# Gated feed-forward of a two-layer block: shifted rows fetched one group ahead, statistics between products, last chunk padded to 128 rows

## What is computed

```python
def shift_token(t):
    t1, t2 = jnp.split(t, 2, axis=-1)
    t2 = jnp.pad(t2, ((0, 0), (1, 0), (0, 0)))[:, :-1]
    return jnp.concatenate([t1, t2], axis=-1)
...
x = x + o @ wo
h = shift_token(x)
mu = h.mean(-1, keepdims=True)
var = h.var(-1, keepdims=True)
h = (h - mu) / jnp.sqrt(var + 1e-05) * lg + lb
h = h @ w1 + b1
a, g = jnp.split(h, 2, axis=-1)
h = a * jax.nn.gelu(g, approximate=False)
x = x + h @ w2 + b2
```

## Time and profile before

| what | value |
|---|---|
| runs | 4908.69, 4929.43, 4920.05 us; median 4920.05 |
| span of the profiled execution | 4908.8 us (its own time is not listed apart; the lowest run is 4908.69) |
| TensorE busy | 4331.1 us, 88% |
| VectorE busy | 2249.6 us, 46% |
| ScalarE busy | 1413.8 us, 29% |
| GpSimd busy | 1258.3 us, 26% |
| mean granted TensorE clock | 0.90 of full |
| DMA | 115.02 MB, 23 GB/s |

### The profile page before, as it was taken

How to read it: one execution, slowest core, us unless ns; L and a number is a source line. 1 busy time by engine, 2 the same in 40 slices (tenths; PEclk the granted TensorE clock), 3 DMA queues, 4 the chain that set the end, 5 groups by cost and what they waited for, 6 DMA issues and landing times. The chain is left out here.

```text
span 4908.8 us, 71554 instructions
## 1 busy us (share of the span) xinstructions
PE 4331.1 (88%) x23249; PEld 2982.9 (61%) x23250; DVE 2249.6 (46%) x5734; ACT 1413.8 (29%) x4622; POOL 1258.3 (26%) x1134
## 2 busy tenths in 40 slices
PE   4999999994996499999998989999687899996875
PEld 3676777762664377777775656676343466764442
DVE  4555555552555334333331156666223466664223
ACT  1333333331111222222222234444111244442111
POOL 2333333333223311111111033343101233432000
PEclk9999999996998578777779989999888999998887
DMA  3000000004001200000001010000100000001003
GB/s 102 2 1 2 1 1 1 2 1 154 30 30 64 89 1 1 1 1 1 1 1 55 17 35 6 9 6 6 55 12 9 28 6 9 6 6 52 12 11 104
DMA packets 102500, 115.02 MB, mean 23 GB/s; under 512 B 11384, under 2 KB 92428, under 8 KB 101516
## 3 DMA queue, kind: packets, MB, share of 16 engines
q1 hardware_dynamic: 97292, 98.38, 6.0%
q0 software_dynamic: 4992, 13.64, 0.8%
HBM read 66.91 MB, written 27.26 MB: 19 GB/s over the span
## 5 line engine op out<-in xcount | busy, mean ns | idle before, releaser
L636 ACT ACTIVATE win_probs<-win_score,win_negmax 128x128 f32<-128x128 f32 (+2 forms) x1170 | 464.1, 405 | 1324.3 <-DVE win_negmax L766 1324.3
L396 POOL TENSOR_TENSOR win_probs<-win_probs,win_rsum 128x512 f32<-128x512 f32 (+1 forms) x420 | 422.7, 1007 | 1465.1 <-DVE win_rsum L781 771.7
L766 DVE TENSOR_REDUCE win_negmax<-win_score 128x2 f32<-128x512 f32 (+2 forms) x422 | 283.0, 671 | 945.5 <-PE win_score L522 479.2
L1498 PE MATMUL ffn_hidden<-ffn_hT,ffn_weights_w 128*128 128x512 f32 x640 | 321.0, 662 | 153.3 <-DVE ffn_inner L1590 151.4
L1779 PE MATMUL rot_lin<-rot_weights_w_qkv,rot_hT 128*128 128x512 f32 x816 | 404.9, 619 | 7.5 <-ACT rot_qk L1875 5.5
L1903 ACT ACTIVATE rot_probs<-rot_probs,rot_negmax 128x256 f32<-128x256 f32 x520 | 260.0, 501 | 366.6 <-DVE rot_negmax L1971 366.6
L1498 PEld LDWEIGHTS ffn_hidden<-ffn_hT,ffn_weights_w 128*128 128x128 f32 x640 | 133.7, 214 | 332.7 <-issue 169.8
L794 DVE COPY win_probsT<-win_turned 128x512 f32<-128x512 f32 (+1 forms) x416 | 276.2, 664 | 93.0 <-PE win_turned L532 92.5
L516 PE MATMUL win_score<-win_KT,win_QT 32*128 32x256 f32 x1036 | 294.4, 403 | 0.0
L1817 PE MATMUL rot_score<-rot_KT,rot_QT 64*128 64x256 f32 x1040 | 292.9, 406 | 0.0
L532 PE MATMUL win_turned<-keep_ident,win_probs 128*128 128x128 f32 x1600 | 287.8, 306 | 0.0
(11 more groups left out here) (271 smaller groups left out, 7912.4 us busy)
## 6 DMA issues: line engine op xcount, KB each, us to landing
weights_w<-in_L_ffn_W SPq DMA_DIRECT2D x16, 512.0 KB
scratch_rows_in<-keep_xn SPq DMA_DIRECT2D x1, 5120.0 KB, 16.5
experts_rows<-scratch_rows_in SPq DMA_DIRECT2D x40, 128.0 KB, 2.0
scratch_rows_out<-experts_y POOLq DMA_DIRECT2D x40, 128.0 KB, 2.0
rot_weights_w_qkv<-in_L_ffn_wqkv SPq DMA_DIRECT2D x3, 1536.0 KB, 6.5
rot_h<-keep_xn SPq DMA_DIRECT2D x36, 128.0 KB
rot_h<-keep_xn SPq DMA_DIRECT2D x36, 127.0 KB
keep_xn<-in_L_attn_x SPq DMA_DIRECT2D x4, 1024.0 KB, 9.4
```

The source lines that it names most:

```text
L396: pool.tensor_tensor(mine, mine, bcast(rsum[:, u % 4, 0:heads], [P, heads, keys]), ALU.mult)\
L636: last = act.activation(probs[:, u % 4, i * width:(i + 1) * width], score[u % 4][:, i * width:(i + 1) * width], ACT.Exp, bias=negmax[:, u ...
L766: dve.tensor_reduce(negmax[:, u % 4, 0:heads], score[u % 4][:, 0:heads * keys].rearrange("p (h k) -> p h k", h=heads), AX.X, ALU.max, nega ...
L1498: last = pe.matmul(hidden[m % RING][k][:], w1[:, c, a:a + P], hT[:, c, :], start=(c == 0), stop=(c == KC - 1))
```

## The change

- The gated weights own a tile `h` for the raw shifted rows (`weights.h`, called `raw` in the stage), beside the stage's `h` for scaled rows. Group 0's rows are fetched by the rotary stage before, on SP, between its last two `after` calls, and that stage waits for them at its end. The fetch of group g is issued once group g-1's rows have been scaled (`h_ready`).
- `make_h` is split: `statistics` of group g+1 (it waits for the fetch) after product 2 of group g (counting from 0), `variances` after product 3, `normalise`, from `raw` to `h`, after the last product and before `take_out`.
- `inner`'s last chunk and `w2`'s last chunk are cleared to 128 rows by GpSimd, once per stage each, and `project` reads 128 partitions in every chunk. SP's load of the 42 rows of `w2` becomes the last of the list and waits for the clear; DVE waits for the clear of `inner` before its first statistics.

The diff, with lines between hunks left out:

```diff
@@ -1341,12 +1341,20 @@
             self.w1_rest = s.sb("w1_rest", [P, KC, P])
+            self.h = s.sb("h", [P, TPG, D])
         self.w2 = s.sb("w2", [P, self.chunks, D])
...
-    def load(self, sp, io, done, layer):
+    def load_h(self, sp, X2, g, done):
+        half = D // 2
+        sp.dma_start(self.h[:, :, 0:half], X2[:, bass.ds(g * TPG + 1, TPG), 0:half]).then_inc(done, 16)
+        sp.dma_start(self.h[1:P, :, half:], X2[0:P - 1, bass.ds(g * TPG + 1, TPG), half:]).then_inc(done, 16)
+        sp.dma_start(self.h[0:1, :, half:], X2[P - 1:P, bass.ds(g * TPG, TPG), half:]).then_inc(done, 16)
+    def load(self, sp, io, done, layer, cleared=None):
@@ -1357,10 +1365,12 @@
         if self.gated:
-            loads += [(self.w2[0:REST, whole, :], at(io[pre + "w2"])[whole * P:, :]),
-                      (self.w1_rest[:, :, 0:REST], w1[:, :, whole * P:self.hid]),
-                      (self.w1_rest[:, :, P // 2:P // 2 + REST], w1[:, :, self.hid + whole * P:])]
-        for dst, src in loads:
+            loads += [(self.w1_rest[:, :, 0:REST], w1[:, :, whole * P:self.hid]),
+                      (self.w1_rest[:, :, P // 2:P // 2 + REST], w1[:, :, self.hid + whole * P:]),
+                      (self.w2[0:REST, whole, :], at(io[pre + "w2"])[whole * P:, :])]
+        for i, (dst, src) in enumerate(loads):
+            if self.gated and i == len(loads) - 1:
+                sp.wait_ge(cleared, 1)
             sp.dma_start(dst, src).then_inc(done, 16)
@@ -1418,7 +1428,7 @@
         w1, w2, b1, b2, gain, offset = weights.w1, weights.w2, weights.b1, weights.b2, weights.gain, weights.offset
-        h = s.sb("h", [P, TPG, D])
+        raw, h = weights.h if gated else X2, s.sb("h", [P, TPG, D])
         hT = s.sb("hT", [P, KC, TOK])
@@ -1428,7 +1438,7 @@
         out = [s.ps(f"out{i}") for i in range(2)]
-        next_loaded, h_loaded = s.sem("next_loaded"), s.sem("h_loaded")
+        next_loaded, h_loaded, cleared = s.sem("next_loaded"), s.sem("h_loaded"), s.sem("cleared")
         var_ready, rstd_ready = s.sem("var_ready"), s.sem("rstd_ready")
@@ -1440,20 +1450,12 @@
             def _(sp):
-                def load_h(g):
-                    half = D // 2
-                    sp.dma_start(h[:, :, 0:half], X2[:, bass.ds(g * TPG + 1, TPG), 0:half]).then_inc(h_loaded, 16)
-                    sp.dma_start(h[1:P, :, half:], X2[0:P - 1, bass.ds(g * TPG + 1, TPG), half:]).then_inc(h_loaded, 16)
-                    sp.dma_start(h[0:1, :, half:], X2[P - 1:P, bass.ds(g * TPG, TPG), half:]).then_inc(h_loaded, 16)
-                if gated:
-                    load_h(0)
                 rotary_loads = rotary.load(sp, io, next_loaded, next_layer)
...
                     with sp.Fori(1, NG) as g:
-                        sp.wait_ge(turned_ready.sem, turned_ready.at(g, 0))
-                        load_h(g)
+                        sp.wait_ge(h_ready.sem, h_ready.at(g, 0))
+                        weights.load_h(sp, X2, g, h_loaded)
+                    sp.wait_ge(h_loaded, 48 * (NG - 1))
                 else:
@@ -1466,6 +1468,7 @@
                 if gated:
+                    pool.memset(inner[:, IC - 1, :], 0.0).then_inc(cleared, 1)
                     with pool.Fori(0, NG) as g:
@@ -1506,7 +1509,7 @@
                             last = pe.matmul(out[n % 2][:, 0:D],
-                                             inner[0:rows[m], m, n * P:(n + 1) * P], w2[0:rows[m], m, :],
+                                             inner[:, m, n * P:(n + 1) * P], w2[:, m, :],
                                              start=(m == 0), stop=(m == IC - 1))
@@ -1558,38 +1561,52 @@
-                def make_h(g, first):
+                def statistics(g, later):
+                    if later:
+                        dve.wait_ge(h_loaded, g * 48)
+                    dve.tensor_scalar(raw[0:1, 0, D // 2:], raw[0:1, 0, D // 2:], keep.going[0:1, bass.ds(g, 1)], None, ALU.mult)
+                    dve.drain()
+                    for n in range(TPG):
+                        dve.bn_stats(stats[:, n, :], raw[:, n, :])
+                def variances():
+                    dve.drain()
+                    for n in range(TPG):
+                        dve.bn_aggr(mv[:, n, :], stats[:, n, :])
+                    dve.drain()
+                    dve.tensor_scalar(ve[:], mv[:, :, 1], 1e-5, None, ALU.add).then_inc(var_ready, 1)
+                def normalise(g, first):
                     if gated:
-                        dve.wait_ge(h_loaded, g * 48 + 48)
-                        dve.tensor_scalar(h[0:1, 0, D // 2:], h[0:1, 0, D // 2:], keep.going[0:1, bass.ds(g, 1)], None, ALU.mult)
-                        dve.drain()
-                        for n in range(TPG):
-                            dve.bn_stats(stats[:, n, :], h[:, n, :])
-                        dve.drain()
-                        for n in range(TPG):
-                            dve.bn_aggr(mv[:, n, :], stats[:, n, :])
-                        dve.drain()
-                        dve.tensor_scalar(ve[:], mv[:, :, 1], 1e-5, None, ALU.add).then_inc(var_ready, 1)
                         dve.wait_ge(rstd_ready, g + 1)
-                        for n in range(TPG):
-                            dve.tensor_scalar(h[:, n, :], h[:, n, :], mv[:, n, 0:1], rs[:, n:n + 1], ALU.subtract, ALU.mult)
-                    else:
-                        if not first:
-                            dve.wait_ge(turned_ready.sem, turned_ready.at(g, 0))
-                        for n in range(TPG):
+                    if not first:
+                        dve.wait_ge(turned_ready.sem, turned_ready.at(g, 0))
+                    for n in range(TPG):
+                        if gated:
+                            dve.tensor_scalar(h[:, n, :], raw[:, n, :], mv[:, n, 0:1], rs[:, n:n + 1], ALU.subtract, ALU.mult)
+                        else:
                             t = g * TPG + n
-                            dve.tensor_scalar(h[:, n, :], X2[:, g * TPG + (n + 1), :], keep.mean[:, bass.ds(t, 1)],
+                            dve.tensor_scalar(h[:, n, :], raw[:, g * TPG + (n + 1), :], keep.mean[:, bass.ds(t, 1)],
                                               keep.rstd[:, bass.ds(t, 1)], ALU.subtract, ALU.mult)
...
-                def multiply(g):
+                def multiply(g, m):
+                    dve.wait_ge(gel_ready.sem, gel_ready.at(g, m + 1))
+                    dve.scalar_tensor_tensor(inner[0:rows[m], m, :], hidden[m % RING][0][0:rows[m], :],
+                                             b1[0:rows[m], 0, m:m + 1], gel[0:rows[m], m % 2, :],
+                                             ALU.add, ALU.mult).then_inc(inner_ready.sem, 1)
+                def multiply_and_prepare(g):
                     for m in range(IC):
-                        dve.wait_ge(gel_ready.sem, gel_ready.at(g, m + 1))
-                        dve.scalar_tensor_tensor(inner[0:rows[m], m, :], hidden[m % RING][0][0:rows[m], :],
-                                                 b1[0:rows[m], 0, m:m + 1], gel[0:rows[m], m % 2, :],
-                                                 ALU.add, ALU.mult).then_inc(inner_ready.sem, 1)
+                        multiply(g, m)
+                        if m == 2:
+                            statistics(g + 1, True)
+                        if m == 3:
+                            variances()
+                    normalise(g + 1, False)
@@ -1606,14 +1623,20 @@
-                make_h(0, True)
+                if gated:
+                    dve.wait_ge(cleared, 1)
+                    statistics(0, False)
+                    variances()
+                normalise(0, True)
                 with dve.Fori(0, NG - 1) as g:
-                    make_h(g + 1, False)
                     if gated:
-                        multiply(g)
+                        multiply_and_prepare(g)
+                    else:
+                        normalise(g + 1, False)
                     take_out(g)
                 if gated:
-                    multiply(NG - 1)
+                    for m in range(IC):
+                        multiply(NG - 1, m)
                 take_out(NG - 1)
@@ -1661,6 +1684,7 @@
         next_loaded, zeroed, masking = s.sem("next_loaded"), s.sem("zeroed"), s.sem("masking")
+        cleared, first_rows = s.sem("cleared"), s.sem("first_rows")
         front_loaded, back_loaded = s.sem("front_loaded"), s.sem("back_loaded")
@@ -1700,7 +1724,7 @@
                 load_h(0, 2, back_loaded)
-                following_loads = following.load(sp, io, next_loaded, layer)
+                following_loads = following.load(sp, io, next_loaded, layer, cleared)
@@ -1717,12 +1741,15 @@
                 after(NG - 2, NG - 1, 0)
+                following.load_h(sp, X2, 0, first_rows)
                 after(NG - 1, 0, None)
+                sp.wait_ge(first_rows, 48)
                 sp.wait_ge(back_loaded, 48 * (NG + 1))
...
             def _(pool):
```

(1 more changed line is left out.)

## The result

The median is 4690.02 us over four runs (4680.42 to 4693.27) against 4921.72 us over four of the kernel before (4908.69 to 4929.43); the ratio is 0.9536, 95% interval 0.9520 to 0.9552. The profiled execution has a span of 4678.7 us, 230.1 less than before.

What follows compares the result with a forecast made beforehand. Bound: TensorE's path in both gated stages, with holes of 151.4 us in one, waiting for DVE's products. Savings of 199.6 in stages plus 30.8 at starts, less 0.5 for semaphores, make 230 us: 4920 - 230 = 4690, range 4662 to 4725.

Steps and rivals of the forecast that it cites:

- Steady group: Gated stages, TensorE: with no hole, a lap is hidden part 18.98, project 10.36 and turn 0.88, 30.2 us.
- Padding: Project's products against w2: reading 128 rows instead of 42 saves 1.41 us a group, 22.6 in 16 groups.
- Rival A: Project's products: the padding gives nothing, 42-row records cost for another reason; laps of 31.6 us, time 4713; chance 0.07.
- First group: Each gated stage's start: group 1's fetch queues behind the rotary tables' loads, readable at 3501; TensorE stalls 3.5 us.
- Last loop group: Each gated stage's end: GpSimd's scaling of rotary tables slows DVE's scaling of rows; TensorE stalls 2.7 us.
- Stage: Each gated stage, TensorE's first transpose to last product: 246.0 + 3.5 + 2.7 = 252.2 us; both 504.4, 199.6 less.
- rival B: Gated stages' first and last groups: stalls of 6 and 4.8 us, each hole dropping the clock; 4711; chance 0.12.
- Start: Start of each gated stage: first fetch moved into the rotary stage, DVE begins 15.4 us earlier, 30.8 for two.
- Rival C: DVE's queue before product 4: waiting for the fetch stalls TensorE once it needs more than 22.6 us; slower; chance 0.02.

Runs made afterwards that it cites:

- rows_100: The changed kernel with the product against w2 reading 100 partitions of the last chunk instead of 128, all still cleared; 4670.8 us, one run.
- rows_64: The changed kernel with the product against w2 reading 64 partitions of the last chunk instead of 128, all still cleared; 4715.0 us, one run.
- no_pad: The changed kernel with the product against w2 reading only the 42 written rows of the last chunk again, clears kept; 4716.1 us (0.9594).
- fetch_before_tables: The changed kernel with group 1's fetch issued ahead of the rotary tables' loads at each gated stage's start; stage sum 498.6 us against 504.3.
- tables_after_rows: The changed kernel with GpSimd's scaling of the rotary tables held until the last group's rows are scaled; stage sum 500.2 us against 504.3.
- fetch_at_start: The changed kernel with group 0's rows fetched at the start of the gated stage again; 4718.8 us (0.9590).
- slow_fetch: The changed kernel with a spare copy of the 127-row transfer ahead of each fetch but the first; 4788.4 us (0.9737).
- 2 x 2: Old or new statistics order, with one tile or own tile, padding and early first fetch kept: old order 4872.2 and 4755.5 us, new order 4687.7 and 4690.0.
- in_place: The changed kernel with one tile for raw and scaled rows, each fetch waiting for the transposes, new order kept; 4687.7 us (0.9538).

## Why the prediction was right

Forecast 4690, range 4662 to 4725, measured 4690.02. That it hits to a fraction of a microsecond is luck: the runs of the changed kernel spread over 13 us, those of the kernel before over 21, and the first gated stage's first transposes come anywhere from 3466.55 us (`rows_100`) to 3487.45 (`rows_64`) in kernels that differ in nothing before it. That it is right to some microseconds is not, since each term stands in the trace:

- *Steady group.* Lap 30.2 forecast, 30.12 measured; hidden part 18.89 instead of the 18.98 taken.
- *Padding.* 22.6 forecast; `no_pad` gives 24.3 by laps and 25.5 of stage. The half of project is 5.18 as worked out; the transposes and the hidden records beside it also run slightly closer (17.33 for 40 records, 17.43 before). The size was right because it was taken as a difference of whole halves. The reason beside it, 0.315 us for each short record against 0.216, makes only 8 x 0.1 = 0.8 of the 1.41 a group; the rest was in the full records next to them. The Trainium skill (TensorE: Matmul & The Clock Gate, "Why this matters for your kernels") says that a single matmul of 32 rows takes as long as one of 128. Within a run of 64-row records the trace agrees, 0.216 us each in `rot_score` as in full ones; at the change between short and full it does not: `rows_64` and `rows_100` differ by 0.67 us a half. Rival A is out.
- *First group.* A hole of 3.5 was forecast from the queueing of the fetch behind the tables, readable at 3501; it was readable at 3501.5, with holes of 2.27 and 1.86. The hole was smaller because TensorE came to it 1.3 us later (3481.44 + 20.26 = 3501.70, forecast 3500.4), mostly by a slower first hidden part, which no term foresaw. But in the first stage the half clock came on top (3.35 us from start to start for four records, 1.72 elsewhere), which the forecast did not have there. `fetch_before_tables` confirms that the tables' loads held the fetch.
- *Last loop group.* 2.7 forecast, 2.60 and 2.59 measured, with DVE's scaling begun 3.3 us after the first of GpSimd's six operations (3.5 forecast); `tables_after_rows` confirms it. The Trainium skill (SBUF — State Buffer, "SBUF: two separate sides") says that GpSimd's instructions and some of VectorE's (those in a two-port mode, or with two SBUF inputs) take a shared port pair as a lock for a whole instruction. By that each of the four short instructions would wait for one of GpSimd's, and 6.27 us against 1.37 agrees; that the scaling is of one of these kinds is not shown by any run here.
- *Stage.* 252.2 forecast, 253.1 and 251.1 measured. Of rival B (worse edges) one part shows, in one stage: the clock drop after a hole, 1.8 us.
- *Start.* 15.4 a stage forecast; DVE's wait fell from 18.09 to 2.79, 15.3. `fetch_at_start` loses it again: TensorE waits 15.5 us longer in a stage, 31 in both, 5 come back in the stages, and the time is 27 us (by the ratios) to 29 (by the medians) longer.
- *Rival C.* The mechanism exists and its point was placed to some 1.5 us (22.6, and 24.1 in the group shown): `slow_fetch` passes it with 27.6 us a fetch and loses 98 us. The kernel's own ordinary fetches stay under it: no DVE wait for one in groups 2 to 7.
- *What the prediction did not see.* It counted the own tile and the order as one change. The 2 x 2 above shows that order alone brings the whole, and that own tile alone brings two thirds (4872 to 4755 of 4872 to 4690). It also had one price for the padding, with and without holes, which was right only because the holes go.

The sum, against spans: 199.7 us of stages, 2 x 15.3 of starts, in all 230.3; the spans differ by 230.1. In this pair of executions, each the fastest of its kernel, the rest of the program adds up to nothing.

## What to carry to other kernels

When an engine's queue holds a wait for a transfer ahead of work that others need, move the wait behind that work before buying a second buffer: here the order alone was worth 184 us, and the buffer nothing more, as long as the transfer (16.8 us to its reader) fits into the work put ahead of the wait (some 24 us). A saving that lies between the point that starts a transfer and the stall that waits for it is given back by the stall, so price such edits with the stall gone. After the large stall is gone, look at the edges: what else is queued when the first transfer goes out, and which engine's bulk work begins as the last group passes.

## What was not expected of the hardware

A hole of the same length sometimes costs the clock and sometimes not. In the changed kernel the hole of 2.27 us was followed by the 1.2 GHz level and the one of 2.60 was not. These are its busy times by stretch (length, PE, PEld, DVE, ACT, POOL, granted clock, DMA share, GB/s):

```profile
3503.00:3505.00 2.00, 1.03 (x2) 0.54 (x3) 1.82 (x8) 0.00 (x0) 0.28 (x1) 0.81 0.02 4
3505.00:3507.00 2.00, 2.00 (x3) 0.77 (x3) 0.33 (x1) 0.00 (x0) 0.72 (x1) 0.50 0.00 0
...
3696.00:3698.00 2.00, 1.86 (x13) 1.76 (x14) 0.81 (x3) 1.16 (x2) 1.32 (x1) 1.00 0.00 0
```

And in `fetch_before_tables`, second stage, the same hole of 2.59 us before the last transposes did cost it, 1.87 us for eight records instead of 1.09, and 6.29 for the half project after it:

```profile
4595.70 1.87 PE L1488 MATMUL ffn_turned<-keep_ident,ffn_h 128*128 128x128 f32 x8 [2.59 <-DVEq L1595]
4597.36 6.29 PE L1514 MATMUL ffn_out<-ffn_weights_w,ffn_inner 128*128 128x256 f32 x24
```

Nor does the length order them: in the first groups, holes of 1.95 to 2.27 us in five of the kernels were followed by slow records, and holes of 2.78 (`in_place`), 2.98 (`no_pad`), 3.06 (`rows_100`) and 3.23 us (`rows_64`) by records at full speed, 1.98 us for four. The hidden part ahead of the first kind had taken 20.3 us, ahead of the second 19.1 to 19.2; but the holes of 1.65 and 1.86 us after one of 20.4 cost nothing either. So a hole of 2 to 3 us is worth its length or up to 1.8 us more, and one profile does not say which. The other surprise is the step between 64 and 100 rows of the padding's section, which is paid at the change between short and full records.
